# Counting above a threshold: a summed compare on VectorE replaced by a plain compare, a fold and identity products on TensorE

## What is computed

```python
scores = jnp.einsum('bhqd,bhkd->bhqk', q, k) * scale
scores = scores * (1.0 + 0.5 * NORADRENALINE)
top_k = max(1, int(s * 0.2))
top_scores = lax.top_k(scores, top_k)[0]
threshold = top_scores[..., -1:]
emphasis = jnp.where(scores >= threshold, 1.0 + 0.3 * DOPAMINE, 1.0)
scores = scores * emphasis
...
probs = jax.nn.softmax(scores, axis=-1)
ctx = jnp.einsum('bhqk,bhkd->bhqd', probs, v)
```

## Time and profile before

| | |
|---|---|
| time before | 3173.97 us, median of 3 runs (3163.5 to 3178.97) |
| profiled execution, its own time | 3173.85 us |
| its span | 3172.5 us |
| busy share PE / DVE / ACT / POOL | 70% / 78% / 46% / 39% |
| mean granted TensorE clock | 0.823 of full speed |

### The profile page before, as it was taken

The page is one execution under the profiler, slowest core; times in us unless marked ns, Lnnn a source line. Parts: engine busy times, 40 slices in busy tenths (PEclk is TensorE's granted clock), DMA queues, the critical chain, the costliest instruction groups (busy, mean ns, idle before and its releaser), DMA issues. The chain is left out here.

```text
span 3172.5 us, 33555 instructions
## 1 busy us (share of the span) xinstructions
PE 2230.1 (70%) x8648; PEld 1159.3 (37%) x8767; DVE 2473.1 (78%) x6145; ACT 1472.9 (46%) x3124; POOL 1231.8 (39%) x1118
## 2 busy tenths in 40 slices
PE   4168775877767777687768778677868778758644
PEld 2025221553235522454225532345325432435213
DVE  5874888869887799978889797889889897853472
ACT  3317613665245733567236732567236743724322
POOL 1020345414453054523545144532535144534461
PEclk7579786998878788897979889788969889869757
DMA  4011113141132212332121312323122321313223
GB/s 98 1 29 28 29 32 93 44 112 59 52 86 59 90 51 62 95 80 71 51 82 63 97 52 62 92 66 97 51 75 68 95 62 46 97 49 105 77 64 92
DMA packets 137460, 215.11 MB, mean 68 GB/s; under 512 B 17873, under 2 KB 57441, under 8 KB 134113
## 3 DMA queue, kind: packets, MB, share of 16 engines
q1 hardware_dynamic: 133088, 203.88, 22.6%
q0 software_dynamic: 4096, 8.40, 1.0%
HBM read 190.06 MB, written 22.15 MB: 67 GB/s over the span
## 5 line engine op out<-in xcount | busy, mean ns | idle before, releaser
L1370 POOL TENSOR_TENSOR gat<-sil,cbs 128x512 f32<-128x512 f32 x256 | 324.6, 1271 | 214.1 <-PE ps_rest L1300 109.6
L1335 ACT ACTIVATE sil<-ps_rest,w_b1T 128x512 f32<-128x512 f32 x256 | 175.5, 687 | 426.9 <-PE ps_rest L1310 405.0
L768 DVE TENSOR_SCALAR_CACHE_REDUCE wmask<-z,tc 128x512 bf16<-128x512 f16 x512 | 349.8, 740 | 30.3 <-ACT z L735 28.3
L1021 PE MATMUL ps_att<-z,Vp 128*32 128x128 f32 x2048 | 280.2, 283 | 46.0 <-DVE z L1093 33.5
L937 POOL TENSOR_SCALAR wmask<-wmask 128x512 bf16<-128x512 bf16 x256 | 164.3, 642 | 375.2 <-DVE wmask L894 369.3
L1310 PE MATMUL ps_rest<-rest_hT,WF 128*128 128x512 f32 x512 | 289.1, 652 | 16.1 <-ACT sil L1335 16.1
L1300 PE MATMUL ps_rest<-gat,WP 128*128 128x512 f32 x512 | 276.9, 625 | 12.2 <-POOL gat L1370 11.6
L1622 POOL TENSOR_TENSOR rest_c<-rest_c,hg 128x512 f32<-128x512 f32 x128 | 162.3, 1268 | 315.4 <-DVE hg L1581 315.4
L1549 ACT ACTIVATE ps_rest<-cols,Aneg 128x512 f32<-128x512 f32 x256 | 175.5, 688 | 225.4 <-DVE hfc L1569 197.6
L1021 PEld LDWEIGHTS ps_att<-z,Vp 128*32 128x32 f32 x2048 | 208.4, 112 | 135.3 <-issue 113.4
L1526 PE MATMUL ps_rest<-hg,ident 128*128 128x512 f32 x256 | 183.8, 808 | 102.9 <-DVE hg L1581 102.6
(11 more groups left out here) (347 smaller groups left out, 4976.5 us busy)
## 6 DMA issues: line engine op xcount, KB each, us to landing
cbs<-spreads SPq DMA_DIRECT2D x128, 256.0 KB, 3.6
ccs<-spreads SPq DMA_DIRECT2D x128, 256.0 KB, 3.3
WF<-in_w SPq DMA_DIRECT2D x64, 256.0 KB, 2.7
WP<-in_w SPq DMA_DIRECT2D x64, 256.0 KB, 2.7
WF<-in_wfc SPq DMA_DIRECT2D x64, 256.0 KB, 2.7
WG<-in_wgate SPq DMA_DIRECT2D x64, 256.0 KB, 3.0
WP<-in_wproj SPq DMA_DIRECT2D x64, 256.0 KB, 3.1
qk<-bounce SPq DMA_DIRECT2D x32, 384.0 KB, 5.8
```

The costliest lines, as they stand in the source:

```text
L768: od.up(dve.tensor_scalar(wmask[:, i, :], z_at[i], tc[:, 0, i:i + 1], None, ALU.is_ge, ALU.add, accum_out=tc[:, 1, i:i + 1]))
L1021: mm = pe.matmul(obank[o:o + 32, a * P:(a + 1) * P], Vp[:, kc, h, :], pT[u][:, kc, :], start=kc == 0, stop=kc == NT - 1)
L1370: weighed0.up(pool.tensor_tensor(gat[m % 2], sil[m % 2], cbs[e % 2][:], ALU.mult))
```

## The change

In each search round DVE now only compares (a mask of 1 and 0 in 16 bits goes to `wmask`, nothing is summed). In the first three rounds, once all tiles of a group (`FOLDS`) are compared, one DVE instruction adds the right halves of their masks to the left halves (256 columns for each tile are left). TensorE then multiplies `wmask` by a 128 x 128 identity, in slices of 32 or 64 columns of each tile, and accumulates the slices in one PSUM bank: of each tile a strip of 32 or 64 partial sums is left. In the last round, whose full masks the choice still needs, nothing is folded and TensorE takes all 512 columns. One DVE reduction for each group sums the strips to counts. ACT's tiles are counted as before. GpSimd builds the identity once. The generator `pe_search` is new and stands last in the attention chain, and that chain's numbers in `weave` go from (453.0, 1.1) to (459.0, 1.25).

```diff
+FOLDS = {18: ((0, 10), (10, 18)), 24: ((0, 16), (16, 24)), 32: ((0, 16), (16, 24), (24, 32))}
+FOLD_W = {16: 32, 12: 32, 10: 32, 8: 64, 6: 64}
...
+    def fold_bank(n):
+        return att.bank[3 - n]
...
+    def pe_search(b):
+
+        for k in range(ROUNDS):
+            for n, (lo, hi) in enumerate(FOLDS[TILES - SIGNS[k]]):
+                if k == 0 and n == 0 and b:
+                    yield attended.at(b - 1)
+                    pe.wait_ge(*attended.at(b - 1))
+                if k == 0 and n == 1:
+                    yield zed.all(b)
+                    pe.wait_ge(*zed.all(b))
+                if k < ROUNDS - 1:
+                    yield halved.at(b, spread_before(k) + n)
+                    pe.wait_ge(*halved.at(b, spread_before(k) + n))
+                else:
+                    yield cut.at(b, cut_before(k) + hi - 1)
+                    pe.wait_ge(*cut.at(b, cut_before(k) + hi - 1))
+                w, wide = FOLD_W[hi - lo], S // 2 if k < ROUNDS - 1 else S
+                to = fold_bank(n)[:, 0:(hi - lo) * w].rearrange("p (i w) -> p i w", w=w)
+                for c in range(wide // w):
+                    mm = pe.matmul(to, ident_bf[:], wmask[:, lo:hi, c * w:(c + 1) * w], start=c == 0, stop=c == wide // w - 1)
+                    if c == wide // w - 1:
+                        spread.up(mm)
+                    yield 0.26
...
-                od.up(dve.tensor_scalar(wmask[:, i, :], z_at[i], tc[:, 0, i:i + 1], None, ALU.is_ge, ALU.add,
-                                        accum_out=tc[:, 1, i:i + 1]))
-                yield 0.67
+                cut.up(dve.tensor_scalar(wmask[:, i, :], z_at[i], tc[:, 0, i:i + 1], None, ALU.is_ge))
+                yield 0.27
+                for lo, hi in FOLDS[TILES - SIGNS[k]] if not last else ():
+                    if i == hi - 1:
+                        yield cut.at(b, cut_before(k) + i)
+                        dve.wait_ge(*cut.at(b, cut_before(k) + i))
+                        halved.up(dve.tensor_tensor(wmask[:, lo:hi, 0:S // 2], wmask[:, lo:hi, 0:S // 2], wmask[:, lo:hi, S // 2:S], ALU.add))
+                        yield 0.1 + (hi - lo) * 0.135
+            for n, (lo, hi) in enumerate(FOLDS[TILES - SIGNS[k]]):
+                w = FOLD_W[hi - lo]
+                yield spread.at(b, spread_before(k) + n)
+                dve.wait_ge(*spread.at(b, spread_before(k) + n))
+                od.up(dve.tensor_reduce(tc[:, 1, lo:hi], fold_bank(n)[:, 0:(hi - lo) * w].rearrange("p (i w) -> p i w", w=w), AX.X, ALU.add))
+                yield 0.66
...
-           (453.0, 1.1, (("pe", pe_choices()), ("act", act_choices()), ("dve", dve_choices()), ("pool", pool_choices()),
+           (459.0, 1.25, (("pe", pe_choices()), ("act", act_choices()), ("dve", dve_choices()), ("pool", pool_choices()),
```

More of the change, by code:

```diff
@@ L117, in emit @@
     zero_bf = sb("zero_bf", [P, S], BF16)
+    ident_bf = sb("ident_bf", [P, P], BF16)
     iota_rev = sb("iota_rev", [P, NT, E])
@@ L136, in emit @@
     loaded, late = sig("loaded", len(EARLY) + 1, 16), sig("late", len(LATER), 16, 30.0)
-    built, hot, cleared = sig("built", 18), sig("hot", 8), sig("cleared", 8 * FULL + 2 * E + 7)
+    built, hot, cleared = sig("built", 20), sig("hot", 8), sig("cleared", 8 * FULL + 2 * E + 7)
     siluc, modp, bop, ready = sig("siluc", 2), sig("modp", 2), sig("bop"), sig("ready", 5)
@@ L235, in emit @@
     aim, signed, counted = sig("aim", ROUNDS), sig("signed", sum(SIGNS)), sig("counted")
+    halved = sig("halved", sum(len(FOLDS[TILES - n]) for n in SIGNS[:-1]))
+    cut, spread = sig("cut", sum(TILES - n for n in SIGNS)), sig("spread", sum(len(FOLDS[TILES - n]) for n in SIGNS))
     tallied, ranked = sig("tallied"), sig("ranked")
@@ L336, in pool_setup @@
         built.up(pool.iota(spare[:], pattern=[[P, PICKS]], base=SLOTS, channel_multiplier=1))
+        built.up(pool.memset(ident_bf[:], 0.0)); pool.wait_ge(*built.at(0, 18))
+        built.up(pool.affine_select(out=ident_bf[:], in_=ident_bf[:], compare_op=ALU.not_equal, fill=1.0, base=0,
+                                    pattern=[[-1, P]], channel_multiplier=1))
     def pool_one_hots():
@@ L752, in act_search, with cut_before, spread_before @@
                 yield 0.73
+    def fold_bank(n):
+        return att.bank[3 - n]
+    def cut_before(k):
+        return sum(TILES - n for n in SIGNS[:k])
+    def spread_before(k):
+        return sum(len(FOLDS[TILES - n]) for n in SIGNS[:k])
+    def pe_search(b):
[20 more added lines that the diff above has]
+                    yield 0.26
     def dve_search(b):
@@ L1941, in sp_attention, with pe_searches @@
             yield from sp_stack(b)
+    def pe_searches():
+        for b in every:
+            yield from pe_search(b)
     def pe_refills():
@@ L2103, in emit @@
                     ("dve", dve_finishes()), ("pool", pool_finishes()), ("sp", sp_finishes()))),
-           (453.0, 1.1, (("pe", pe_choices()), ("act", act_choices()), ("dve", dve_choices()), ("pool", pool_choices()),
+           (459.0, 1.25, (("pe", pe_choices()), ("act", act_choices()), ("dve", dve_choices()), ("pool", pool_choices()),
                          ("pe", pe_attention()), ("act", act_attention()), ("dve", dve_attention()), ("pool", pool_attention()),
-                         ("sp", sp_attention()), ("pe", pe_prepares()), ("act", act_prepares()), ("dve", dve_prepares()), ("pe", pe_refills()), ("act", act_refills())))),
+                         ("sp", sp_attention()), ("pe", pe_prepares()), ("act", act_prepares()), ("dve", dve_prepares()), ("pe", pe_refills()), ("act", act_refills()), ("pe", pe_searches())))),
           (("sp", sp_rows()), ("sp", sp_ups()), ("sp", sp_downs())))
```

## The result

The changed kernel takes 3389.34 us (median of 4 runs, 3379.76 to 3389.62), the kernel before 3174.52 beside it (the 3173.97 of the table ahead of the prediction is the median of three of the same four runs). The ratio is 1.0675, with a 95% interval from 1.0642 to 1.0708. The forecast was 3113.

A forecast was written before the change was run, and what follows sets the result against it. DVE was taken as the bound, busy 84% of the middle. With DVE relieved of a net 90 us, head 293, middle 2332 and tail 487 gave 3112, stated as 3113 us, 1.9% less; range 3025 to 3200.

The forecast's parts named there:

- the sum's density: DVE's busy share of the middle, lowered from 0.842 to 0.826 for new waits between DVE and TensorE, about 45 us.
- the middle: Stretch from the end of b = 0's attention to the end of b = 7's: 2496 us before, forecast 2332.
- head and tail: Stretches before the end of b = 0's attention and after the end of b = 7's: forecast 293 and 487 us.
- a tail longer by 111 us: Mamba and states of b = 6 moving behind the last attention: tail from 376 to 487 us.
- Removed counts and compares: On DVE, 736 summing counts (491 us) go; 736 compares of about 344 ns, 199 us in all, replace them.
- Folds and reductions: New DVE work over all sequences: 48 folds at 76 us and 72 PSUM bank reductions at 41 us.
- POOL's port: New compares and folds on DVE stand still while a POOL instruction runs: about 85 us lost.
- Rival B: Compares and folds each wait 0.25 us on average for POOL, 196 us in all; total 3197 us, chance 0.13.
- PE: 544 added identity products on TensorE, between 117 and 237 us, taken as 150.
- rival C: In-order waits on DVE and PE around the reductions push DVE's middle density to 0.80; total 3188 us, chance 0.09.
- Sign for a slowdown: Attention of b = 7 ending later than 2690 instead of near 2625, so that the longer tail outweighs everything.
- Relieved of a net 90: DVE's work over the whole kernel: 175 us saved by the new search, less 85 lost to POOL.

The follow-up runs named there:

- e3: The changed kernel in the same order, with Tanh in place of Silu in the experts of block 0: 3316.05 us.
- e12: e1 with Tanh in place of Silu in the experts of block 0, as a control for e3: 3143.0 us.
- e1: The changed kernel with the attention's two `weave` numbers put back to 453.0 and 1.1: 3140.74 us, ratio 0.9908 to the kernel before.
- e2: The kernel before, old search kept, with only the two `weave` numbers changed to 459.0 and 1.25: 3316.9 us.
- e5: The changed kernel with 440.0 instead of 459.0 as the attention's work in `weave`, lead still 1.25: 3120.14 us.
- e9: e3 without folds, identity products, reductions and their waits, the counts set to constants: 3252.98 us.
- e8: e1 without folds, identity products, reductions and their waits, the counts set to constants: 3100.72 us.

## Why the prediction was wrong

**The step that failed** is the sum's density: "let DVE's density in the middle fall from 0.842 to 0.826, about 45 us". It came out at 0.727, which made the middle 304 us longer than forecast; head and tail were 3 and 25 us shorter, and that is the whole miss of 276 us. I had read the new order on three places of DVE and PE and priced the shift between the chains as a tail longer by 111 us, paid back by 85 us of DVE work that leaves the middle. I had not read ACT's order, which held 178 table loads against 34 before it ran, nor followed the shift through the eight sequences. Ahead of the softmax's first DVE instruction alone DVE idled 232 us more than before. Of the 276 us the runs assign 73 to the tables (after against e3) and 173 to the rest of the shift (e3 against e12), together 246. The other 30 are e12's 3143 against the forecast: the search with the old numbers (e1) gained 33 us, where my sum had 61 with the new ones.

**What the 173 us are** is only partly settled. That the order from the numbers makes them, and neither the search nor the tables, is shown by e2, e5 and e12. Where they lie is shown by e3 and e12: 107 us in the middle, 70 in the tail, and 148 us more of DVE's waiting for the softmax's scores from TensorE. The longer tail I had priced; that the middle grows, instead of shrinking with the work that leaves it, I had not. Why is argued: stages which leave DVE idle stand together, while those that want it stand together too. The windows agree with this (27 us of DVE in a softmax of 118), and e9 against e8 supports it with 23 us. How much of the 173 is this bunching and how much the waits of in-order queues was not told apart.

Two things stay open beside it. TensorE's granted clock was lower in the drifting order, 0.818 in e3 against 0.849 in e12 over the whole run. For the same 9311 products PE was busy 2364.1 us in e3 and 2331.0 in e1, so by that estimate the clock itself carries no more than some 33 us of the 173, and whether it is cause or consequence of the idle time no run tells. Nor is it settled why lead 1.3 suits the new search and not the old one, with 34 loads in each.

**Point by point.**
- Removed counts and compares: right. 345 ns against the forecast 344; the copy and cast rows were the right neighbours.
- Folds and reductions: right. The longest fold is 2.44 us (2.3 forecast), the sum of both 118 us (117).
- POOL's port: right in kind, oversized. The mean compare took 420 ns against a median of 345, which makes 55 us over the 736; the sum had 85 with the folds. It depends on what stands beside the search: in e5, where no states do, the longest compare on z was 543 ns and the same reckoning gives 3 us. Rival B was not the cause.
- PE: busy 116 us more, forecast 150; that is the lower of its two bounds, 117.
- Trip over PE (rival C): 36.2 us of waiting before the reductions in 31 places of the changed kernel, 1.2 us a time where rival C's sign was over 1.5. In e1 it was 64.1 us in 37 places, 1.7 a time. Its number, 0.80 of density, was closer than mine for e1 (1953.80 / 2454 = 0.796), but e8 shows that taking trip, folds and reductions away gives 40 us in all.
- Sign for a slowdown: the attention of b = 7 was to end later than 2690; it ended at 2926. That sign held, for a reason that stood in none of the rivals.
- "Relieved of a net 90": DVE's busy time fell by 133. The relief is real, its worth was the error.
- The rivals lacked the one that came: an order in which the softmax meets the experts on ACT and in TensorE's queue.

## What to carry to other kernels

When a change makes a planner write the order anew, the order is the change: compare the whole queues of every engine, ScalarE's function table loads first (they can be counted before a run), and follow one pair of stages from the first to the last iteration, since a slow drift is worst at the end. If a planner balances two chains by declared work, compare that with what its own costs add up to: 459.0 for 438.6 made the drift. Taking the drift out is not a gain by itself. With a lead of 1.25 the exact work gave the old kernel 2.7% with no other edit, but with a lead of 1.1 it was slower than 453.0 for both searches (3223 against 3174 us, 3242 against 3141). So stop the drift first, then find the lead by measurement. And test a new part at several phases of the schedule before believing in it: its effect here went from -3.3% to +2.2%.

## What the runs showed of the hardware

- A table load takes 1283 ns, minimum, median and maximum alike (157 loads at L1102 and L1387), and the function behind it starts 1.30 us after the load's start (2838.42 and 2839.72 above). The Trainium skill, "ScalarE: Activation LUTs", section "What ACT_TABLE_LOAD costs", names the same 1283 ns and adds a drain of about 1380, 2.66 us for each switch. The trace here shows no such drain in ACT's timeline. A switch cost 0.51 us of the kernel's time on average (e3), less than its own length; ACT was busy only 49% of the span, so that a part of the loads can have fallen into its idle time.
- A 16-bit compare with a per-row operand and no accumulator takes 345 ns for 512 columns, less than half of the 741 of the form that also sums. It can stand still behind a GpSimd instruction: the longest here, 1372 ns, ran from 1332.14 to 1333.51 us, and POOL's L1661 from 1332.09 to 1333.36. The summing form never took more than 748 ns in 736 instances.
- The 16-bit fold with 4096 columns of result took at most 2436 ns, 0.59 ns a column.
